# Layer 0 of a four-layer attention program: attention probabilities turned in 32x32 blocks by VectorE instead of by TensorE

## The reference, cut to what matters

```python
def _L0_xattn_ref(x_this, x_other, Wg, bg, Wtheta, btheta, Wphi, bphi, Wz, bz, gamma, beta):
    g_x = jnp.einsum('oc,bct->bto', Wg, x_this) + bg
    theta = jnp.einsum('oc,bct->bot', Wtheta, x_this) + btheta[None, :, None]
    phi = jnp.einsum('oc,bct->bot', Wphi, x_other) + bphi[None, :, None]
    f = jnp.einsum('bci,bcj->bij', phi, theta)
    f_div_C = jax.nn.softmax(f, axis=-1)
    y = jnp.einsum('bij,bjo->bio', f_div_C, g_x)
    w_y = jnp.einsum('oc,btc->bot', Wz, y) + bz[None, :, None]
    mean = jnp.mean(w_y, axis=(0, 2), keepdims=True)
    var = jnp.var(w_y, axis=(0, 2), keepdims=True)
    w_y = gamma[None, :, None] * (w_y - mean) * jax.lax.rsqrt(var + EPS) + beta[None, :, None]
    return w_y + x_this
```

## Time and profile before

| | us |
|---|---|
| three runs, median (lowest to highest) | 2391.65 (2390.55 to 2395.41) |
| the profiled execution | 2392.45 |
| its span | 2390.7 |
| layer 0: first matmul, and last instruction before layer 1's first load | 7.8 to 197.6 |
| granted clock, mean over the span | 0.975 |

### The profile page before, as it was taken

How to read it: one execution, slowest core, us unless ns; L and a number is a source line. 1 busy time by engine, 2 the same in 40 slices (tenths; PEclk the granted TensorE clock), 3 DMA queues, 4 the chain that set the end, 5 groups by cost and what they waited for, 6 DMA issues and landing times. The chain is left out here.

```text
span 2390.7 us, 57498 instructions
## 1 busy us (share of the span) xinstructions
PE 2244.4 (94%) x22784; PEld 1637.0 (68%) x22784; DVE 1078.3 (45%) x3052; ACT 1087.6 (45%) x3441; POOL 580.0 (24%) x605
## 2 busy tenths in 40 slices
PE   7886999999999999999957999999999999999986
PEld 3444776676777777766546777777777777777754
DVE  4662322222222222222144565566665555666642
ACT  4553333333333333333223465566655655666554
POOL 0000100000000000000034444434444443344420
PEclk9997999999999999999978999999999999999998
DMA  4532000000000000000141001111010111110100
GB/s 163 171 105 64 16 19 19 19 19 19 19 19 19 19 19 19 19 10 5 76 133 21 16 21 26 22 26 22 21 26 16 26 26 22 26 21 16 21 20 10
DMA packets 116698, 81.94 MB, mean 34 GB/s; under 512 B 79136, under 2 KB 91808, under 8 KB 114208
## 3 DMA queue, kind: packets, MB, share of 16 engines
q1 hardware_dynamic: 106240, 48.35, 8.0%
q10 hardware_dynamic: 8032, 18.35, 2.2%
q0 software_dynamic: 2240, 12.58, 1.6%
HBM read 62.49 MB, written 12.58 MB: 31 GB/s over the span
## 5 line engine op out<-in xcount | busy, mean ns | idle before, releaser
L751 PEld LDWEIGHTS bank<-normedT,mlp_w 128*128 128x128 f32 x2048 | 235.0, 193 | 18.1 <-issue 17.1
L751 PE MATMUL bank<-normedT,mlp_w 128*128 128x128 f32 x2048 | 241.0, 278 | 0.8 <-DVE normedT L981 0.8
L761 PE MATMUL bank<-mlp_w,geluT 128*128 128x512 f32 x512 | 228.9, 596 | 0.0
L932 DVE CUSTOM_DVE_ANT_0 probs<-quad,neg_mask 128x256 f32<-128x256 f32 x256 | 90.8, 420 | 275.1 <-PE quad L681 275.1
L1975 ACT ACTIVATE scores<-scores,nmax 128x128 f32<-128x128 f32 x512 | 198.3, 396 | 2.5 <-DVE nmax L2237 2.5
L1463 POOL TENSOR_TENSOR k_even_odd<-k_even_odd,decay_products 128x512 f32<-128x512 f32 x80 | 98.1, 1227 | 328.1 <-PE quad L1659 251.6
L939 DVE COPY probsT<-quad 128x512 f32<-128x512 f32 x128 | 84.8, 683 | 191.6 <-PE quad L695 191.2
L761 PEld LDWEIGHTS bank<-mlp_w,geluT 128*128 128x128 f32 x512 | 93.8, 190 | 103.3 <-issue 103.3
L867 ACT ACTIVATE geluT<-bank,cols 128x128 f32<-128x128 f32 x256 | 73.0, 368 | 177.3 <-PE bank L751 177.3
L1391 POOL TENSOR_TENSOR gn_rstd<-gn_var_eps,halfs 128x32 f32<-128x32 f32 x16 | 87.0, 5435 | 170.2 <-DVE gn_var_eps L2160 170.2
L875 ACT ACTIVATE probs<-probs,nmax 128x256 f32<-128x256 f32 x256 | 126.1, 494 | 2.0 <-DVE nmax L932 1.8
(11 more groups left out here) (246 smaller groups left out, 4559.0 us busy)
## 6 DMA issues: line engine op xcount, KB each, us to landing
x_in<-in_x SPq DMA_DIRECT2D x32, 256.0 KB, 2.9
mlp_w<-in_mlp_w POOLq DMA_DIRECT2D x8, 1024.0 KB, 5.6
ctx_in<-in_ctx SPq DMA_DIRECT2D x16, 256.0 KB, 2.9
l_out<-wy ACTq DMA_DIRECT2D x16, 256.0 KB, 2.3
wy_in<-l_out SPq DMA_DIRECT2D x16, 256.0 KB, 3.5
hT<-in_ctxT SPq DMA_DIRECT2D x16, 256.0 KB, 3.5
l_out<-l_x ACTq DMA_DIRECT2D x16, 256.0 KB, 2.1
x_in<-l_out SPq DMA_DIRECT2D x16, 256.0 KB, 2.5
```

Source lines behind the costliest of these rows:

```text
L751: mm = nc.tensor.matmul(PS[b][:, f * P:(f + 1) * P], mlp_w1[:, c, m * P:(m + 1) * P], nT[:, c, :], start=(c == 0), stop=(c == NC - 1))
L761: mm = nc.tensor.matmul(PS[M.bank][:, :], gT[:, f, :], mlp_w2[:, f, :], start=(f == 0), stop=(f == NF - 1))
L932: mx = nc.vector.tensor_tensor_reduce(probs[:, h, :], PS[b][:, e * 256:(e + 1) * 256], negm[:, :], -1.0 / D1, 3.0e38, ALU.add, ALU.min, nm ...
```

## The change

- The sixteen TensorE transposes and the four copies out of PSUM go. VectorE makes `turn(i, c)` in their place: it transposes each 32x32 block of a chunk of the probabilities, SBUF to SBUF, into `turned`. In `turned`, row group `r` of the partitions (32 partitions) holds 32 keys of each block `j`, for the 32 queries with index `r` in each chunk `c`.
- `out_y` is 64 products of 32 keys, 64 output rows and 128 queries (4 chunks x 32): for each of 16 key blocks `j` one on each of the four row groups, into four PSUM banks, on column half `j % 2`.
- Each row group needs g of all keys on its own 32 partitions, so `g_proj` makes it four times: 64 products with K = 128, 32 output rows, 64 columns, into two banks. The copy of g by ScalarE is 128x1024 in place of 128x256.
- `copy_y` reads the four banks and puts the queries back in order.
- x, the context and g have two buffers each; the inputs of batches 0 and 1 are loaded at the start, later ones when `g_proj(i - 2)` is done.
- TensorE's order in a batch is now: scores (0, 1), theta and phi of the next batch, y of the batch before, scores (2, 3), g of the next batch, z of the batch before. On TensorE, ScalarE and SyncE the loop is written out; `copy_z` is done one batch later than before.

```diff
-        xin = sb("x_in", [P, D])
-        cin = sb("ctx_in", [P, D])
+        xin = [sb(f"x_both{n}", [P, D]) for n in range(2)]
+        cin = [sb(f"ctx_both{n}", [P, D]) for n in range(2)]
-        g = sb("g", [P, NC, CI])
+        g = [sb(f"g_repeated{n}", [P, NB, CI]) for n in range(2)]
-        probsT = sb("probsT", [P, NC, D])
+        turned = sb("probs_turned", [P, NB, NC, SB])
...
-        rings = dict(tp=([4, 5], 2), g=([6], 1), f=([0, 1], 4), t=([2], 2), u=([3], 2), o=([7], 2))
+        rings = dict(tp=([4, 5], 2), f=([6, 7], 4), g=([2], 1), y=([0], 1), z=([0], 1))
...
                 def g_proj(i):
-                    for j in range(NC):
-                        mm = nc.tensor.matmul(PS[b][:, j * CI:(j + 1) * CI], xin[:, j * P:(j + 1) * P], w0[:, 2 * P:2 * P + CI],
-                                              start=True, stop=True)
+                    if i > 1:
+                        pe.wait_ge(Y.free, Y.read(i - 2, 1))
+                    for j in range(NB):
+                        for r in range(RG):
+                            at = j % 8 * CI
+                            mm = nc.tensor.matmul(PS[b + j // 8][SB * r:SB * r + SB, at:at + CI], xin[i % 2][:, j * SB:(j + 1) * SB],
+                                                  w0[:, 2 * P:2 * P + CI], start=True, stop=True)
...
                 def out_y(i):
-                    pe.wait_ge(G.free, G.read(i, 1))
-                    pe.wait_ge(T.free, T.read(i, 2))
-                    pe.wait_ge(U.free, U.read(i, 2))
-                    for j in range(NC // 2):
-                        for n in range(2):
-                            k = n * NC // 2 + j
-                            mm = nc.tensor.matmul(PS[b][n * HALF:(n + 1) * HALF, :], g[:, k, :], probsT[:, k, :],
-                                                  start=(j == 0), stop=(j == NC // 2 - 1))
+                    pe.wait_ge(Y.free, Y.count)
+                    if i > 0:
+                        pe.wait_ge(Z.free, Z.read(i - 1, 1))
+                    pe.wait_ge(G.free, G.read(min(i + 1, B - 1), 1))
+                    pe.wait_ge(s_turned, NC * (i + 1))
+                    for j in range(NB):
+                        n = j % 2
+                        for r in range(RG):
+                            rr = slice(SB * r, SB * r + SB)
+                            mm = nc.tensor.matmul(PS[r][n * HALF:(n + 1) * HALF, 0:P], g[i % 2][rr, j, :],
+                                                  turned[rr, j, :, :].rearrange("p c i -> p (c i)"), start=(j < 2), stop=(j >= NB - 2))
...
+                for i in range(B):
                     scores(i, (0, 1))
+                    if i + 1 < B:
+                        theta_phi(i + 1)
+                    if i > 0:
+                        out_y(i - 1)
                     scores(i, (2, 3))
+                    if i + 1 < B:
+                        g_proj(i + 1)
+                    if i > 0:
+                        out_z(i - 1)
...
+                def turn(i, c):
+                    dve.wait_ge(s_norm, NC * i + c + 1)
+                    if c == 0 and (not isinstance(i, int) or i > 0):
+                        dve.wait_ge(Y.ready, Y.written(i - 1, 1))
+                    nc.vector.transpose(turned[:, :, c, :], probs[:, c, :].rearrange("p (b j) -> p b j", j=SB)).then_inc(s_turned, 1)
...
+                def batch(i, stats=True):
                     maximum(i, 0)
                     maximum(i, 1)
                     normalise(i, 0)
                     normalise(i, 1)
+                    if stats:
                         statistics(i - 2)
+                    turn(i, 0)
+                    turn(i, 1)
                     maximum(i, 2)
                     maximum(i, 3)
                     normalise(i, 2)
+                    turn(i, 2)
                     normalise(i, 3)
+                    turn(i, 3)
```

More of the change, by code:

```diff
@@ L89, in end, with layer0 @@
         assert self.n == self.per_batch, f"per_batch should be {self.n}"
[L92 removed]
+def layer0(nc, a, PS, quad, sem, C, cols, rows, rows1, ident, hsum, halfs, s_const, s_ident, bn_scale, bn_shift, l0_out,
            weights1, s_w1):
+    SB = 32
+    NB = D // SB
+    RG = P // SB
     with ExitStack() as ctx:
@@ L119, in layer0 @@
         s_w0 = sem("l0_weights_loaded")
-        s_in = sem("l0_inputs_loaded")
+        s_in = [sem(f"l0_inputs_loaded{n}") for n in range(2)]
         s_nmax = sem("l0_max_ready")
@@ L152, in _ @@
                     sp.dma_start(wz[n * HALF:(n + 1) * HALF, :], a["wz"][0:CI, :]).then_inc(s_w0, 16)
+                load(1)
                 sp.dma_start(hsum[:, :], a["hsum"]).then_inc(s_hsum, 16)
@@ L155, in _ @@
                 sp.dma_start(rows1[:, :, :], a["rows1"].unsqueeze(0).to_broadcast([P, ROWS1, D])).then_inc(s_hsum, 16)
-                with sp.Fori(1, B) as i:
-                    sp.wait_ge(G.ready, G.written(i - 1, 1))
+                for i in range(2, B):
+                    sp.wait_ge(G.ready, G.written(i - 2, 1))
                     load(i)
@@ L220, in scores @@
                             .then_inc(F.ready, 1)
[L222 to L233, removed]
@@ L249, in out_z @@
-                def out_z(i):
[L250 to L253, removed]
+                def out_y(i):
+                    Y.begin(i)
+                    Y.next()
+                    pe.wait_ge(Y.free, Y.count)
[9 more added lines that the diff above has]
+                                                  turned[rr, j, :, :].rearrange("p c i -> p (c i)"), start=(j < 2), stop=(j >= NB - 2))
+                    mm.then_inc(Y.ready, 1)
@@ L255, in _ @@
+                def out_z(i):
+                    Z.begin(i)
+                    b = Z.next()
+                    pe.wait_ge(Z.free, Z.count)
+                    pe.wait_ge(Y.free, Y.read(i, 1))
+                    nc.tensor.matmul(PS[b][:, :], wz[:, :], y[:, :], start=True, stop=True).then_inc(Z.ready, 1)
                 theta_phi(0)
                 g_proj(0)
[L257 to L262, removed]
+                for i in range(B):
@@ L282, in _ @@
             def _(act):
-                TP, G, F, U, O = (ring(k) for k in ("tp", "g", "f", "u", "o"))
+                TP, G, F, Y, Z = (ring(k) for k in ("tp", "g", "f", "y", "z"))
                 act.wait_ge(s_const, 48)
@@ L289, in theta @@
                     act.wait_ge(TP.ready, TP.count)
+                    if i > 0:
+                        act.wait_ge(F.ready, F.written(i - 1, NC))
                     nc.scalar.activation(thetaT[:, :], PS[b][:, :], ACT.Identity, bias=bias2[:, 0:1]).then_inc(TP.free, 1)
@@ L340, in _ @@
                 phi(0)
-                copy_g(0)
-                exp(0, 0)
-                exp(0, 1)
-                exp(0, 2)
-                exp(0, 3)
-                theta(1)
-                phi(1)
-                def batch(i, last=False):
+                for i in range(B):
+                    copy_g(i)
+                    if i > 1:
+                        copy_z(i - 2)
                     exp(i, 0)
-                    copy_probsT3(i - 1)
                     exp(i, 1)
-                    copy_y(i - 1)
-                    copy_g(i)
-                    if not last:
+                    if i > 0:
+                        copy_y(i - 1)
+                    if i + 1 < B:
                         theta(i + 1)
@@ L359, in batch @@
                     exp(i, 3)
-                    copy_z(i - 1)
-                batch(1)
-                with act.Fori(2, B - 1) as i:
-                    batch(i)
-                batch(B - 1, True)
-                copy_probsT3(B - 1)
+                copy_z(B - 2)
                 copy_y(B - 1)
```

87 lines of the change are left out of this document (24 added, 63 removed).

## The result

The changed kernel takes 2382.37 us (median of 6 runs, 2379.75 to 2384.57); the kernel before, beside it, 2391.27 (6 runs, 2390.55 to 2395.41). The profiled execution took 2381.2 us, with a span of 2379.4, 11.3 less than the 2390.7 of before. So the sign is right, the time lies in the range, and two thirds of the gain are missing.

What follows compares the result with a forecast made beforehand. TensorE, with one hole, bounds layer 0 at 10.93 us a batch; at 9.1, 14 batches save 25.6, start adds 0.5, end saves 0.6: -25.7 us from 2392.45 profiled (median 2391.65), say 2367, range 2358 to 2389.

Steps and rivals of the forecast that it cites:

- the sign: Whole kernel: the change makes it faster, by 25.7 us; faster by more than can be told, chance 0.78.
- Nothing for the rest: Layer 0's doubled inputs, moved loads and written-out loops: no time gained or lost; DMA share from 0.52 to 0.62.
- TensorE, 8.81: TensorE's sum per layer 0 batch: 4.85 us unchanged steps, 1.84 for g, 2.12 for y.
- The chain at 8.96: VectorE's operations and waits from one batch's first transpose to the next's: 8.96 us, each transpose taken at 0.69.
- ScalarE's copy of g: Layer 0 on ScalarE: the larger copy takes some 1.3 us and is covered; uncovered, at most 0.9 more.
- Start and end: Layer 0's edges: y of batch 0 ends 0.5 us later, at about 29.4; the end takes 0.6 less.
- The doubled inputs: Two buffers each for x and context in layer 0: no TensorE row waits for a load, so nothing saved.
- A: Rival, layer 0: slower y or transpose, or engines missing each other; batch 9.5 to 10.5 us, 2372 to 2386; chance 0.17.
- B: Rival, y on TensorE: column halves don't overlap; y 4.0 us, TensorE's sum 10.7, about 2390; chance 0.07.
- C: Rival, y on TensorE: weight loads wait for the other half's product; y 6.4 us, batch 13.1, 2426; chance 0.04.
- D: Rival, VectorE: a float32 block transpose takes two passes, 1.37 us; batch 11.7, 2402; chance 0.09.
- E: Rival, TensorE in layer 0: small tiles lose the clock; half speed, batch 17.6 us, 90 more; chance 0.02.

Runs made afterwards that it cites:

- e10: The changed kernel with TensorE's batches 2 to 13 as a loop of six passes over two batches, nothing else; 2367.97 us, ratio 0.9901.
- e1: The kernel before with only TensorE's loop over the batches of layer 0 written out; 2390.89 us, ratio 1.0003.
- e3: The changed kernel with g made by 34 matmuls in place of 64, y taking the blocks in the resulting order; 2373.34 us, ratio 0.9932.
- e4: The changed kernel with g by 34 matmuls and z ahead of g, between y and g; 2365.87 us, ratio 0.9899.
- e6: The changed kernel with 128 raises of an unused semaphore at the head of TensorE's program; 2399.52 us, ratio 1.0032.
- e5: The changed kernel with layer 1's weight loads held back behind all inputs of layer 0; one run, 2389.34 us, with layer 1 waiting for weights.
- e8: e4 with VectorE's block transpose of chunk 1 done twice in each batch; 2373.38 us, ratio 0.9923.
- e7: e4 with one buffer each for x and the context in place of two; 2423.73 us, ratio 1.0132.
- e9: e4 with TensorE's batches 2 to 13 as a loop of six passes over two batches; 2365.85 us, ratio 0.9895.

## Why the prediction was right and wrong

**The step that failed** is the last sentence of "Nothing for the rest": "The written-out loops only add instructions." It is a term taken at nothing, and it measured 14.4 us (the changed kernel less e10). Without it the forecast holds: e10 is 23.7 us below the kernel before that ran beside it, where 24.7 was forecast. The size fits the missing part: from the start of y of batch 0 (24.54) to y of batch 14 (167.17) a batch took 142.6 / 14 = 10.19 us where 9.1 was forecast, 15.2 us in 14 batches. Of these 11.4 are idle time; some 1.6 are the lower clock behind the stop of 1.98 (z at 163.41 takes 2.00 in place of 1.06, the scores behind it 1.76 in place of 1.06, with a granted clock of 0.51 and 0.59); the rest lies in bursts that run slower than 16 ns a record without a visible gap (y from 86.50 takes 2.55 to the scores, an undisturbed one 2.02, at a granted clock of 1.00) and in the 9.2 of some batches. What carries the cause, one by one: e10 takes only the writing-out away, and the stops and most of the loads go; e1 adds only the writing-out, and nothing stops; e3 thins out the code, and the stops become rarer, and in e4, with the two bursts also further apart, they vanish; e6 moves them with the code; e5 clears the weights. The size of the code could be read from the order of the changed kernel beforehand; that nothing in the old layer 0 was both written out and dense was the warning.

**TensorE, 8.81**: 9.04 in e10, right within 3%. y took 2.02 (2.12 forecast from the 32-column form), g 1.92 (1.84). The missing 0.23 is in steps that do not change: theta and phi 1.91 from start to start in place of 1.82, z 1.06 in place of 0.91, with other neighbours than before; no run took these apart.

**VectorE**: the block transpose takes 0.711, the forecast was 0.69. The chain at 8.96 is close: e8 gives 8.8. In the forecast it set the batch by 0.15; in fact TensorE does, by a little. ScalarE's copy of g takes 1.03 (1.3 forecast) and is covered.

**Start and end**: y of batch 0 ends at 26.57, 2.8 before the 29.4 of the forecast and 2.35 before the kernel before. The first g cost 2.76 from start to start (11.44 to 14.20), not 3.7, since only its first 36 matmul records ran slowly (some 314 ns each, the later ones 219), the second g ran in time that TensorE had waited in before (18.64 to 21.00), and y then stood ready behind theta and phi, at 24.54. The forecast had priced the first g at half speed throughout and let y wait for the chain behind exp 3. It called that half clock; the granted clock reads 1.00 there in both kernels, so why the first matmuls are slow stays open. At the end y of batch 15 was done 9.1 us behind y of batch 14 (170.69 to 176.49 + 3.34) where 9.4 was forecast. So of layer 0's 12.2 us, 2.35 come from the start, 153.0 - 144.1 = 8.9 from the 14 batches (end of y to end of y, a stop of 1.10 in the last one among it), 0.9 from the end.

**The doubled inputs**, "they save nothing": true of the old order, where nobody waited for a load; in the new order they carry everything, 57.9 us in e7. The term of the sum was right, since the change has them; the reason given was for another order.

**The rivals.** A, "something in between", has the time (2372 to 2386) and a batch of 10.19, but by luck, for it came by none of the causes that it named: y at 3 us came about in single batches, by the stops, not by its tiles. B and C are refuted: y's column halves work beside each other on the same rows, 128 records in 2.02 us, 16 ns each, with a weight load in every one. So the rule that a load overlaps only where its row group differs (the Trainium skill, "TensorE: Matmul & The Clock Gate", Part 3) is not what bounds y here. D would have needed a transpose of 1.18 us. E would have needed a lower clock in the loop, and its mean was 0.99; it fell only behind a stop, at the end.

**What stays open.** Not every 256th instruction costs. In the changed kernel the big stops, up to 1.98 us, stand 1.4 us or more behind the start of a burst (records 86 to 125; in e3, with longer records, 53 to 55; one, of 1.01, in the z right behind g); at earlier places there is 0.4 us or nothing, and at late ones it varies too (0.52 in y behind record 108, 1.86 in g behind 103, nothing in y behind 117 and in g behind 112). The two longest of all, in e5, came while the DMA engines were busy throughout; whether other transfers explain the rest too, no run here shows. Nor does one show when a load is asked for, or how much code stays at hand; only that the 1,090 or so instructions of the loop do.

## What to carry to other kernels

- When a change writes a loop out or puts small tiles in place of large ones, count the instructions of each engine and its rate. Here two bursts of 256 instructions in 2 us each, written out for every batch, cost 14.4 us more than the same code with twelve of the 16 batches in a loop, and the loop has no stop (e10); sparse code may be written out for free (e1).
- A gap "issue" in the middle of a run of equal instructions is no dependence that the profile shows. Note behind which record it falls in successive rounds: a constant step, together with an instruction queue that moves bytes, points to code being loaded, and filler instructions at the head of the program, which move the places, test it (e6).
- Both cures work: fewer instructions for the same work, with sparse work between the bursts (e4, 2365.9; e3, without the latter, 2373.3), or a loop (e10, 2368.0; both together, e9, 2365.9). Either is 1.0% faster than the kernel before, the changed kernel 0.4%.

## What the runs showed of the hardware that was not expected

- Instructions arrive in pieces of some 16 KB (0.43 MB in 26 loads), by the step of the stops 256 instructions, and in two written-out bursts of 256 in 2 us each they can be late: stops of 0.2 to 2.55 us, and of 4.7 us while other transfers kept the DMA engines busy throughout (e5).
- Behind the stop of 1.98 us the granted clock was 0.51 and 0.59 for 3.8 us (163.41 to 167.17; 1.2 GHz is 0.5) and z and the scores went at about half speed; behind those of 1.86 and 1.73 it stayed at 1.00.
- In the loop no such stops and, from 53 to 134 us, no loads, though its 1,090 or so instructions are over four pieces.
- 128 semaphore raises on TensorE took 19.6 us, 0.15 each, at the start of the program.
- Beside bursts of small tiles the large products took longer than before, from start to start: 0.09 for theta and phi together, 0.15 for z. No run takes this apart.
